# Last stage of a fused attention and feed-forward kernel: the next front product behind the first gate and up product, its rows turned a body sooner, new orders on ScalarE and VectorE

## The reference, cut to what matters

```python
def h_bitlinear(x, w):
    xq = act_quant(fwht(x))          # Walsh-Hadamard transform, then 8 bit by the row's largest magnitude
    wq = weight_quant(w)             # -1, 0, 1 times a scale
    return jnp.einsum('bsh,oh->bso', xq, wq)
gate = h_bitlinear(hidden_states, w_gate)     # 512 -> 2048
up = h_bitlinear(hidden_states, w_up)         # 512 -> 2048
return h_bitlinear(jax.nn.silu(gate) * up, w_down)   # 2048 -> 512
...
x = x + _L1_ffn_ref(_layernorm(x, axis=-1), ...)
```

## Time and profile before

| what | value |
|---|---|
| median of 3 runs | 712.64 us (712.16 to 714.21) |
| the profiled execution | 712.6 us, of which the span is 710.7 us |
| TensorE busy | 648.1 us (91%) |
| VectorE busy | 585.5 us (82%) |
| ScalarE busy | 471.2 us (66%) |
| GpSimd busy | 363.2 us (51%) |
| mean granted clock of TensorE | 0.993 of full |
| last stage | from about 444 us to the end |

### The profile page before, as it was taken

How to read it: one execution, slowest core, us unless ns; L and a number is a source line. 1 busy time by engine, 2 the same in 40 slices (tenths; PEclk the granted TensorE clock), 3 DMA queues, 4 the chain that set the end, 5 groups by cost and what they waited for, 6 DMA issues and landing times.

```text
span 710.7 us, 12362 instructions
## 1 busy us (share of the span) xinstructions
PE 648.1 (91%) x4055; PEld 375.2 (53%) x4086; DVE 585.5 (82%) x1331; ACT 471.2 (66%) x965; POOL 363.2 (51%) x277
## 2 busy tenths in 40 slices
PE   1689799999999999997999999897999999999996
PEld 0366466757666666763444444453545555545543
DVE  6889899999999888357788975787888888888775
ACT  3747467766776655477687841576878888778734
POOL 2022132322222313157676730068999999899970
PEclk9999999999999999999999999999999999999999
DMA  8981223343331332708999941354566755665621
GB/s 216 244 270 23 81 83 98 97 97 99 82 104 31 107 73 67 252 16 199 301 257 302 217 110 23 64 85 75 106 127 110 132 119 103 138 128 114 109 60 45
DMA packets 173130, 88.21 MB, mean 124 GB/s; under 512 B 150546, under 2 KB 152594, under 8 KB 172052
## 3 DMA queue, kind: packets, MB, share of 16 engines
q1 hardware_dynamic: 167188, 71.94, 44.5%
q10 hardware_dynamic: 3408, 11.27, 4.8%
q0 software_dynamic: 2480, 4.33, 3.4%
HBM read 51.20 MB, written 4.19 MB: 78 GB/s over the span
## 4 chain that ended last, share of the span: by engine, by line
DVE 32%; PE 30%; issue 12%; ACT 10%; POOL 6%; DMA 5%; SPq 3%; DVEq 0%; POOLq 0%; ACTq 0%
PE ps L1734 7%; PE ps L1829 6%; PE ps L1811 5%; DMA arena<-arena 5%; PE ps L1749 4%; DVE y_sm L1557 4%; PE ps L1887 3%; DVE X L1143 3%; DVE arena L1234 2%; POOL arena L559 2%; POOL arena L560 2%; DVE ps L1517 2%; ACT arena L924 2%; PE ps L1686 2%; ACT arena L907 2%
## 5 line engine op out<-in xcount | busy, mean ns | idle before, releaser
L1734 PE MATMUL ps<-arena 128*128 128x256 f16 x1408 | 160.1, 273 | 10.2 <-DVE arena L1234 6.8
L1734 PEld LDWEIGHTS ps<-arena 128*128 128x128 f16 x1408 | 135.5, 98 | 36.0 <-DVE arena L1234 10.4
L487 POOL TENSOR_TENSOR arena<-arena 128x256 f16<-128x256 f32 x88 | 57.6, 673 | 181.6 <-ACT arena L662 181.1
L1887 PE MATMUL ps<-arena 128*128 128x512 bf16 x486 | 115.6, 380 | 7.5 <-ACT arena L876 4.0
L559 POOL TENSOR_TENSOR arena<-arena 128x1024 f32<-128x1024 f32 x44 | 103.7, 2356 | 31.9 <-DVE arena L1531 26.9
L560 POOL TENSOR_TENSOR arena<-arena 128x1024 f32<-128x1024 f32 x44 | 103.9, 2360 | 0.0
L1749 PE MATMUL ps<-arena 128*128 128x512 f16 x352 | 80.3, 385 | 3.6 <-POOL arena L487 3.5
L1887 PEld LDWEIGHTS ps<-arena 128*128 128x128 bf16 x512 | 47.9, 98 | 65.1 <-DVE arena L1523 8.0
L655 ACT ACTIVATE arena<-ps,gs 128x256 f32<-128x256 f32 x88 | 40.7, 466 | 51.8 <-PE ps L1734 51.7
L1829 PE MATMUL ps<-arena 128*128 128x512 f16 x256 | 59.4, 387 | 5.7 <-issue 3.6
L1959 PE MATMUL ps<-arena 128*128 128x512 bf16 x251 | 59.1, 379 | 2.0 <-ACT arena L954 1.8
(11 more groups left out here) (167 smaller groups left out, 1188.6 us busy)
## 6 DMA issues: line engine op xcount, KB each, us to landing
arena<-in_ctx_t SPq DMA_DIRECT2D x7, 1024.0 KB, 5.9
arena<-in_wg_t SPq DMA_DIRECT2D x16, 256.0 KB, 3.9
arena<-in_wu_t SPq DMA_DIRECT2D x16, 256.0 KB, 4.3
arena<-in_wd_t SPq DMA_DIRECT2D x16, 256.0 KB, 4.8
arena<-in_ctx_n SPq DMA_DIRECT2D x4, 1024.0 KB, 10.9
arena<-in_wu_t ACTq DMA_DIRECT2D x4, 1024.0 KB, 5.9
arena<-in_wd_t ACTq DMA_DIRECT2D x4, 1024.0 KB, 5.7
out_x<-X SPq DMA_DIRECT2D x16, 256.0 KB, 2.5
```

The source lines that it names most:

```text
L487: nc.gpsimd.tensor_tensor(hl[:, c, at:at + 2 * P], b_h[n % 4], hh[:, c, at:at + 2 * P], ALU.subtract).then_inc(b_hl_r, 1)
L1734: last = M(bank(n % 2)[:, 2 * P * i:2 * P * i + 2 * P], W[:, b, c * P:c * P + P], part[:, b, at:at + 2 * P], start=(b == 0 and part is xhT ...
L1887: last = M(bank(2 * (n % 2) + i), d_qT[u][:, b, :], W[:, b, D * n:D * n + D], start=(b == 0), stop=(b == KD - 1))
```

## The change: the orders of one body on three engines

No instruction is added or taken away, and GpSimd and SyncE are as before. On TensorE `d_front(k + 1)` goes from ahead of `gate_up(k, 2)` to behind `gate_up(k, 0)`, where `d_turn(k + 1)` stood; `q_turn(k + 1)` goes ahead of `gate_up(k, 2)`; `d_turn` is now that of tile k + 2 and stands behind `h_product(k - 1, 2)`. ScalarE and VectorE get new orders for the whole body: `d_high`, `d_low` and `d_normal` of one tile later, `d_round`, `d_turned` and `front_scales` early in the body, `odd_evac(k - 1, 2)` and `(k - 1, 3)` at the end of the same body instead of at the start of the next, and on VectorE both first stages of tile k - 2 ahead of the first `back_max`, and `d_residual` ahead of `d_hidden(k, 3)`. Body 0 gets pieces of its own, since the front of tile 2 has to start there.

```diff
@@ -956,49 +956,52 @@
 
             def d_body(k, u):
                 w = 1 - u
-                front, mid, whole, back, rounding, ahead = on(k + 1), on(k), on(k) and not at(k, NT - 1), on(k - 1), on(k - 3), on(k + 2) and not (at(k, 0) or at(k, 1))
-                if on(k - 2):
-                    odd_evac(k - 2, 2)
-                    odd_evac(k - 2, 3)
+                front, mid, whole, back, rounding, next_turn, ahead = on(k + 1), on(k), on(k) and not at(k, NT - 1), on(k - 1), on(k - 3), on(k + 2), on(k + 3) and not at(k, 0)
                 if mid:
                     d_silu(k, u, 0)
+                if whole:
+                    d_hi(k, 0)
                 if front and not at(k, 0):
-                    d_high(k + 1)
+                    d_round(k + 1, w)
                 if mid:
                     d_silu(k, u, 1)
                 if whole:
-                    d_hi(k, 0)
-                if rounding:
-                    y_round(k - 3, w, 0)
-                if whole:
                     d_hi(k, 1)
-                if rounding:
-                    y_whole(k - 3, 0)
                 if back:
                     odd_evac(k - 1, 0)
                     odd_evac(k - 1, 1)
-                if mid:
-                    d_silu(k, u, 2)
-                if front:
-                    d_round(k + 1, w)
-                if whole:
-                    d_hi(k, 2)
+                if rounding:
+                    y_round(k - 3, w, 0)
+                if front and not at(k, 0):
+                    d_turned(k + 1, w)
                 if rounding:
                     y_round(k - 3, w, 1)
                 if mid:
+                    d_silu(k, u, 2)
+                if at(k, 0):
+                    d_round(1, w)
+                if rounding:
+                    y_whole(k - 3, 0)
+                if whole:
+                    d_hi(k, 2)
+                if mid:
                     d_silu(k, u, 3)
-                if front:
-                    d_turned(k + 1, w)
-                if ahead:
-                    d_normal(k + 2, u)
+                if next_turn and not at(k, 0):
+                    d_high(k + 2)
+                if at(k, 0):
+                    d_turned(1, w)
+                    d_high(2)
                 if whole:
                     d_hi(k, 3)
+                if back:
+                    odd_evac(k - 1, 2)
+                    odd_evac(k - 1, 3)
+                if ahead:
+                    d_normal(k + 3, w)
                 if rounding:
                     y_whole(k - 3, 1)
 
             def d_drain():
-                odd_evac(14, 2)
-                odd_evac(14, 3)
                 for n in range(4):
                     h_evac(n)
                 last_odd_evac(0)
@@ -1013,7 +1016,7 @@
                     for n in range(2):
                         yq_evac(j, n)
 
-            tiles(act, d_body, 1, 3, 0, NT)
+            tiles(act, d_body, 3, 3, 0, NT)
             d_drain()
 
 
@@ -1580,24 +1583,24 @@
 
             def d_body(k, u):
                 w = 1 - u
-                front, mid, whole, back, rounding, out_part = on(k + 1), on(k), on(k) and not at(k, NT - 1), on(k - 1), on(k - 3), on(k - 4)
-                if rounding:
-                    back_max(k - 3, w, 0)
+                front, mid, whole, back, rounding, out_part, next_turn = on(k + 1), on(k), on(k) and not at(k, NT - 1), on(k - 1), on(k - 3), on(k - 4), on(k + 2)
                 if on(k - 2):
                     first_stage(k - 2, 2)
                     first_stage(k - 2, 3)
                 if rounding:
-                    back_max(k - 3, w, 1)
+                    back_max(k - 3, w, 0)
                 if mid:
                     d_hidden(k, u, 0)
                 if front and not at(k, 0):
-                    d_low(k + 1)
+                    front_scales(k + 1, w)
+                if whole:
+                    d_lo(k, 0)
+                if rounding:
+                    back_max(k - 3, w, 1)
+                if mid:
+                    d_hidden(k, u, 1)
                 if rounding:
                     back_scales(k - 3, w)
-                if mid:
-                    d_hidden(k, u, 1)
-                if whole:
-                    d_lo(k, 0)
                 if at(k, 0):
                     dve.wait_ge(c_add, NT)
                     d_stats(NT - 2)
@@ -1605,24 +1608,27 @@
                     d_variances(1)
                 if whole:
                     d_lo(k, 1)
-                if front:
-                    front_scales(k + 1, w)
+                if at(k, 0):
+                    front_scales(1, w)
                 if back:
                     first_stage(k - 1, 0)
+                    first_stage(k - 1, 1)
                 if mid:
                     d_hidden(k, u, 2)
-                if back:
-                    first_stage(k - 1, 1)
                 if whole:
                     d_lo(k, 2)
                 if at(k, 1):
                     d_shifts(1)
+                if out_part:
+                    d_residual(k - 4, u)
                 if mid:
                     d_hidden(k, u, 3)
-                if out_part:
-                    d_residual(k - 4, u)
+                if next_turn and not at(k, 0):
+                    d_low(k + 2)
                 if whole:
                     d_lo(k, 3)
+                if at(k, 0):
+                    d_low(2)
 
             def d_drain():
                 first_stage(14, 2)
@@ -1962,11 +1968,11 @@
 
             def d_body(k, u):
                 w = 1 - u
-                front, mid, back, out_part = on(k + 1), on(k), on(k - 1), on(k - 4)
+                front, mid, back, out_part, next_turn = on(k + 1), on(k), on(k - 1), on(k - 4), on(k + 2)
                 if mid and not at(k, 0):
                     gate_up(k, u, 0)
                 if front and not at(k, 0):
-                    d_turn(k + 1, w)
+                    d_front(k + 1)
                 if mid:
                     gate_up(k, u, 1)
                 if back:
@@ -1974,19 +1980,25 @@
                     h_product(k - 1, 1)
                 if out_part:
                     down(k - 4, u, 0, 8)
-                if front:
-                    d_front(k + 1)
+                if at(k, 0):
+                    d_front(1)
+                if front and not at(k, 0):
+                    q_turn(k + 1)
                 if mid:
                     gate_up(k, u, 2)
                     gate_up(k, u, 3)
                 if back:
                     h_product(k - 1, 2)
-                if front:
-                    q_turn(k + 1)
+                if at(k, 0):
+                    q_turn(1)
+                if next_turn and not at(k, 0):
+                    d_turn(k + 2, u)
                 if out_part:
                     down(k - 4, u, 8, 16)
                 if back:
                     h_product(k - 1, 3)
+                if at(k, 0):
+                    d_turn(2, u)
 
             def d_drain():
                 for n in range(4):
@@ -2003,7 +2015,7 @@
                     yq_turn(j)
                     down(j, j % 2)
 
-            tiles(pe, d_body, 1, 4, 0, NT)
+            tiles(pe, d_body, 2, 4, 0, NT)
             d_drain()
 
 
```

## The result

The changed kernel takes 724.7 us (median of 6 runs, 723.11 to 729.78) against 713.78 us for the kernel before (median of 6): ratio 1.0158, 95% interval 1.0128 to 1.0189. It is slower, as forecast: 722.9 was predicted, 10.3 more than before, and the two medians lie 10.9 apart. The profiled execution took 723.11 us with a span of 721.1 us (forecast 721.0, that is 710.7 + 10.3).

A forecast was written before the change was run, and what follows sets the result against it. A closed chain across in-order ScalarE and VectorE was taken as the bound, growing from 15.11 to 16.0 us a body: +2.5 start, +10.3 over eleven bodies, -2.5 end, on 712.6 gives 722.9 us; own range 719.5 to 725.5.

The forecast's parts named there:

- 3: butterflies, maximum: VectorE, next body: two first stages and back_max, the same three as today in another order, 2.45 us.
- 4: d_hidden(0) to the second maximum: VectorE: d_hidden(0) 0.67, front_scales 1.22, d_lo(0) 0.61 and second back_max 1.12 us.
- 6: third silu and hidden product: ScalarE to VectorE: d_silu(2) 0.69, hand-off 0.03, d_hidden(2) 0.76 and 0.05, together 1.53 us.
- step 5: VectorE's d_hidden(1) 0.80, then ScalarE's d_hi(1) 0.48, odd_evac pair 0.66, y_round 1.05, d_turned 0.48, y_round 1.05.
- Start: Last stage's start: GpSimd's tile 0 later by +0.6, +1.0 and +0.7, at 471.2; body 4's first maximum +2.5 us.
- End: Last stage's end: GpSimd starts tile 13 0.1 behind body 15's maximum instead of 2.6, -2.5 us.
- The front product's wait for d_low: TensorE: d_low made a body sooner, so this wait goes from the list or falls under 0.1; worth nothing by itself.
- SyncE's transposes at nothing: SyncE: y_whole's second-half transposes precede the second hidden half's; taken at nothing, else 0 to about 1 us a body.
- Rival A: Loop bodies: TensorE decides and the new orders keep up, 14.56 a body, 706.6 us; 10%.
- Rival B: Loop bodies: the closed chain over down and the residual decides, 15.5 a body, 717.4 us; 14%.
- Rival C: Whole kernel: gain and loss cancel or the period stays 15.1, within 0.3% of before, 713 us; 6%.
- Rival D: TensorE: gaps grow to about 1.4 us a body and its clock falls, near 728 us; 8%.

The follow-up runs named there:

- a_best: Changed kernel with its TensorE order kept and ScalarE and VectorE reordered: 709.39 us, ratio to the kernel before 0.9935 to 0.9982.
- a_yround_late: Changed kernel with ScalarE's second y_round moved from ahead of the third silu to behind d_hi(2): 721.37 us.
- d_best: Kernel before with reordered ScalarE and VectorE, including first stages ahead of the first maximum and the odd_evac pair behind d_hi(3) of the body before: 705.91 us.
- b_ kernels: Kernel before with one edit set each: shorter down 717.4 us; second y_round early and d_normal late 709.13; those plus odd_evac(k - 1, 1) behind d_round 708.23.
- c_best: Kernel before with second y_round early, d_normal and odd_evac(k - 1, 1) later, and both first stages ahead of the first back_max: 718.43 us.
- a_ kernels: Changed kernel with edits to ScalarE's or VectorE's order, a shorter down, or both: 709.39 to 723.57 us.

## Why the prediction was right, step by step

The mechanism held: a closed chain over ScalarE and VectorE sets the bodies, and the new order makes it longer. By its steps, start to start in the trace of after:

| steps | predicted us | measured us |
|---|---|---|
| 1, 2: d_hidden(3), d_hi(3), d_lo(3) | 0.80 + 0.63 + 0.61 = 2.04 | 578.24 - 576.22 = 2.02 |
| 3: butterflies, maximum | 2.45 | 580.69 - 578.24 = 2.45 |
| 4: d_hidden(0) to the second maximum | 3.62 | 584.29 - 580.69 = 3.60 |
| 5: d_hidden(1) to the third silu | 4.52 | 588.65 - 584.29 = 4.36 |
| 6: third silu and hidden product | 1.53 | 590.18 - 588.65 = 1.53 |
| 7: d_hi(2), d_lo(2), d_residual | 1.90 | 592.08 - 590.18 = 1.90 |
| sum | 16.06 | 15.86 |

- **The odd_evac pair in step 5 was mis-sized.** I took 0.66 and gave 0.53 as its lower end; it is 586.09 - 585.57 = 0.52. Its 0.66 in the earlier trace rows was the distance to a silu with other operands to wait for, not the pair's cost. The bodies fell inside 15.8 to 16.2, and the eleven of them cost (674.73 - 500.26) - (662.82 - 497.09) = 8.7 instead of 10.3.
- **Start**: measured from the stage's start, GpSimd's first tile is 471.98 - 444.58 - (468.87 - 443.90) = 2.4 later, body 4's maximum 2.5 later; predicted 2.3 and 2.5. How the 2.3 divides over its three parts was not measured; the wait of body 3's odd_evac for GpSimd, on which the 2.5 rests, is there (1.07 us, ending at 491.05).
- **End**: -1.5 instead of -2.5. GpSimd did start tile 13 0.16 behind the maximum instead of 2.61. But "GpSimd's two tiles set the end as today" failed. Before, GpSimd and VectorE were ready for tile 15's butterfly at the same moment (689.2). After, GpSimd was done at 698.67, and VectorE, which had waited for ScalarE and that for TensorE, started only at 699.66. Before, and then after:

```profile
686.83 2.37 POOL L560 TENSOR_TENSOR arena<-arena 128x1024 f32<-128x1024 f32 x1
...
689.24 1.22 DVE L1549 TENSOR_TENSOR arena<-arena 128x1024 f32<-128x1024 f32 x1
...
696.31 2.36 POOL L560 TENSOR_TENSOR arena<-arena 128x1024 f32<-128x1024 f32 x1
697.82 0.60 ACT L941 ACTIVATE arena<-ps 128x512 f32<-128x512 f32 x1 [3.62 <-PE ps L1942]
...
698.45 0.69 DVE L1541 TENSOR_TENSOR arena<-ps,arena 128x512 f32<-128x512 f32 x1 [2.13 <-ACT arena L941]
...
699.66 1.22 DVE L1552 TENSOR_TENSOR arena<-arena 128x1024 f32<-128x1024 f32 x1
```

- **The sum** is 2.5 + 8.7 - 1.5 = 9.7 in the stage and 0.7 ahead of it, which the change doesn't touch. That the forecast span of 721.0 met 721.1 to 0.1 is luck: errors of about -1.6 and +1.0 and this 0.7 cancelled; the terms are good to 1.6 us, not to 0.1.
- **The front product's wait for d_low is not gone**: 4.0 us in 8 bodies, as before (3.8). I had argued that d_low is made a body sooner; but the front product stands sooner too, and d_low(k + 2) sits behind the late fourth hidden product (576.88), ending at 577.56. Nothing followed from it for the time, since TensorE is not in the chain.
- **SyncE's transposes at nothing** held: no wait of the list names a DMA, and their users have no idle time ahead of them.
- **Rival A** (TensorE decides) is refuted for both kernels by the two runs with a short down: by matmul busy time TensorE led, and taking 1.3 us of its work away moved the period by 0.01. The Trainium skill, page Perfetto Trace Analysis, section Identifying the Most-Contended Engine, says to optimize the engine with the highest occupancy first, but to judge the headroom of TensorE by its matmul FLOPs or by the busy share of its weight loads. Neither way of ranking finds what set the period here: by matmul busy time TensorE leads, by its weight loads (9.9 of 20 us before, 9.4 after) it is last, and GpSimd, the highest of the others before (18.8 of 20), waited 0.8 us a tile for VectorE. Rival A becomes true in a_best, where the period of 14.55 is its 14.56 and TensorE has no wait left.
- **Rival B** was real, but second: a_yround_late brought it out at 15.57, against 15.5.
- **Rival C** (no difference) is refuted: the interval of the ratio, 1.0128 to 1.0189, leaves out 1.
- **Rival D**: the mean clock is 0.995, no lower than before (0.993), and 1.00 in the loop.

The cause of the loss is thus shown, and not only argued: two edits inside the chain moved the period by what the walk of the chain gives (0.16 for the residual, and 0.67 for the y_round once the second chain was out of the way), 1.3 us less of TensorE's work did not move it, the parallel chain came out at 15.57 and was gone with a shorter down, and a_best takes the loss away with the change's TensorE order kept.

And the move of the front product itself? a_best (new place) and d_best (old place) have the same period: once the other engines keep up, the new place gains nothing in the bodies. At the start it costs: counted from the stage's start GpSimd's first tile begins at 25.0 to 25.1 us in the kernels with the old order of TensorE (before, all b_ kernels, c_best, d_best) and at 27.4 to 27.7 in those with the new one (after and all a_ kernels). How much of these 2.4 to 2.6 us is the front product's place alone stays open, since ScalarE's and VectorE's orders at the start differ too.

## What to carry to other kernels

With in-order engines that hand to each other, look for the longest closed chain of one period, with start-to-start distances, and not for the busiest engine; then for the second longest, since it caps what shortening the first is worth (a move worth 0.67 us in the first chain gave 0.29). Count also what a moved instruction costs where it lands: 1.04 us taken out of one step put 0.35 back into another. A move on one engine can be half an edit: the first stages' new place cost 0.92 us a body until their producer on the other engine moved too. And compare a stage by its own length where the part ahead of it varies.

## What the runs showed of the hardware

The unchanged part ahead of the last stage took from 443.4 to 449.1 us in the profiled executions, up to 5.7 us of difference with no change in it. Two short instructions on ScalarE cost less than they last: in the loop of after the pair L936, 0.38 to 0.39 us each, has its follower start 0.52 us after its own start. A hand-off between ScalarE and VectorE took 0.03 to 0.04 us in either direction there, from listed end to start (585.04 to 585.07, 589.35 to 589.39, 590.15 to 590.18, 590.78 to 590.82).
